# An attention GNN on one core: h joins the ff sum by transposes between the first down products, b2 as a 128-row product, and the mask's diagonal as a column

## The reference, cut to what matters

```python
x0 = relu(layernorm(x))                      # L0's input
mask = adj + eye(n) > 0
for l in range(3):
    scores = leaky(si[:, :, None] + sj[:, None, :] + attn_b[l], 0.2)   # si = x @ w[:d], sj = x @ w[d:]
    attn = softmax(where(mask, scores, -inf))
    h = layernorm(x + attn @ x, g1[l], beta1[l])
    ff = gelu(h @ W1[l] + b1[l]) @ W2[l] + b2[l]                       # hidden width 1024
    x = layernorm(h + ff, g2[l], beta2[l])
x = x_in + x
h = relu(layernorm(x)); Wh = h @ W
e = where(adj > 0, leaky(s_i[:, :, None] + s_j[:, None, :], 0.2), -9e15)   # without the eye
out = x + leaky(softmax(e, axis=1) @ Wh)
```

## Time and profile before

| | |
|---|---|
| median of 3 runs | 2426.69 us |
| span of the profiled execution | 2423.8 us (no time of its own is given for it; the median lies 2.9 us above its span) |
| TensorE busy | 2089.5 us, 86% |
| VectorE busy | 1850.2 us, 76% |
| ACT busy | 1086.6 us, 45% |
| GpSimd busy | 926.1 us, 38% |
| DMA | 52.85 MB, mean 22 GB/s |

### The profile page before, as it was taken

The page is one execution under the profiler, slowest core; times in us unless marked ns, Lnnn a source line. Parts: engine busy times, 40 slices in busy tenths (PEclk is TensorE's granted clock), DMA queues, the critical chain, the costliest instruction groups (busy, mean ns, idle before and its releaser), DMA issues.

```text
span 2423.8 us, 34901 instructions
## 1 busy us (share of the span) xinstructions
PE 2089.5 (86%) x11649; PEld 1778.6 (73%) x11649; DVE 1850.2 (76%) x4984; ACT 1086.6 (45%) x1668; POOL 926.1 (38%) x658
## 2 busy tenths in 40 slices
PE   3898888988899988999889988899888998889894
PEld 2777677877778766877767776778767786778783
DVE  6777887778787787777878778786788768877755
ACT  3444454434454445534444444544445444544341
POOL 2444433443344343343334333343334334333442
PEclk9899999999999999989999899989989999899997
DMA  4001100001000010000100010000100001000000
GB/s 139 18 18 44 43 4 12 14 18 44 11 18 1 18 44 11 18 1 27 36 10 18 1 53 11 10 18 8 46 10 9 18 18 40 5 13 23 1 1 18
DMA packets 40522, 52.85 MB, mean 22 GB/s; under 512 B 2906, under 2 KB 30852, under 8 KB 40324
## 3 DMA queue, kind: packets, MB, share of 16 engines
q1 hardware_dynamic: 40324, 50.37, 6.5%
HBM read 41.97 MB, written 8.39 MB: 21 GB/s over the span
## 4 chain that ended last, share of the span: by engine, by line
issue 34%; PE 27%; DVE 21%; POOL 15%; ACT 2%; DMA 0%; POOLq 0%; SPq 0%; DVEq 0%; ACTq 0%
PE ps_a L400 8%; PE ps_d L469 7%; PE ps_u L439 6%; POOL gelu_lo L1158 5%; DVE h_last L815 4%; DVE h_last L817 4%; POOL rstd L1125 3%; DVE normed L922 3%; PE ps_a L499 2%; POOL probs L1164 2%; PE ps_t L357 2%; DVE probs L966 2%; POOL normed L1141 1%; POOL x_res L1143 1%; POOL x_res L1150 1%
## 5 line engine op out<-in xcount | busy, mean ns | idle before, releaser
L666 ACT ACTIVATE g_full<-ps_u,vec_col 128x512 f32<-128x512 f32 x384 | 259.2, 687 | 782.5 <-PE ps_u L439 349.6
L469 PE MATMUL ps_d<-w_hi,gelu_hi 128*128 128x256 f32 x1536 | 483.4, 315 | 1.2 <-DVE gelu_lo L902 1.1
L469 PE MATMUL ps_d<-w_lo,gelu_hi 128*128 128x256 f32 x1536 | 458.3, 298 | 0.0
L469 PE MATMUL ps_d<-w_hi,gelu_lo 128*128 128x256 f32 x1536 | 457.6, 298 | 0.0
L1125 POOL TENSOR_TENSOR rstd<-var_eps,minus_half 128x4 f32<-128x4 f32 x128 | 136.9, 1069 | 683.4 <-DVE var_eps L787 683.4
L400 PE MATMUL ps_a<-x_nat,probs 128*128 128x257 f32 x1536 | 365.8, 390 | 32.6 <-DVE normed L869 27.7
L1158 POOL TENSOR_TENSOR gelu_lo<-g_full,gelu_hi 128x512 fp32r<-128x512 f32 x240 | 318.7, 1337 | 171.4 <-ACT gelu_hi L674 161.8
L400 PEld LDWEIGHTS ps_a<-x_nat,probs 128*128 128x128 f32 x1536 | 285.0, 191 | 106.8 <-DVE normed L869 34.1
L469 PEld LDWEIGHTS ps_d<-w_hi,gelu_hi 128*128 128x128 f32 x1536 | 320.7, 209 | 19.1 <-DVE gelu_lo L902 3.8
L469 PEld LDWEIGHTS ps_d<-w_lo,gelu_hi 128*128 128x128 f32 x1536 | 322.4, 210 | 7.0
L469 PEld LDWEIGHTS ps_d<-w_hi,gelu_lo 128*128 128x128 f32 x1536 | 321.5, 209 | 0.0
(11 more groups left out here) (133 smaller groups left out, 4223.8 us busy)
## 6 DMA issues: line engine op xcount, KB each, us to landing
adj_in<-adj_dram SPq DMA_DIRECT2D x64, 256.0 KB, 3.1
x_nat<-x_dram SPq DMA_DIRECT2D x16, 512.0 KB, 4.1
x_res<-x_dram SPq DMA_DIRECT2D x16, 512.0 KB, 4.0
out_dram<-x_res SPq DMA_DIRECT2D x64, 128.0 KB, 1.7
x_res<-L_gnn_W_dram SPq DMA_DIRECT2D x5, 1024.0 KB, 5.6
probs<-L_gnn_W_dram SPq DMA_DIRECT2D x1, 1024.0 KB, 8.9
attn_row<-L_gnn_attn_w_dram SPq DMA_DIRECT2D x1, 768.0 KB
g_row<-L_gnn_g_dram SPq DMA_DIRECT2D x1, 384.0 KB
```

The lines of the kernel that those rows point to most:

```text
L469: last = pe.matmul(ps_d[c // 2][:, cols:cols + D], h[:, r, tok], w[:, layer, f, :], start=False, stop=(f == FC - 1 and i == 2), skip_group ...
L666: full = act.activation(g_full[:, f % 2, :], ps_u[f % 2][:, :], ACT.Gelu, bias=b1_col[:, layer, f:f + 1])
```

## The change

`residual` becomes one chunk's work and is called between the chunks of the first down product, behind the wait for gelu_lo. h comes from h_full by two transposes (f32, one pass each). ones_r and b2_parts have 128 rows, of which two are not zero in ones_r. The diagonal's transposes and copies go; VectorE takes the diagonal as a column instead, by a multiply-reduce with the identity, clears it by a multiply, and final_mask adds it back. A column of side 1 is kept by a copy in slots (2,1). `junk` gets memory of its own.

```diff
-        b2_parts = sb("b2_parts", [2, LAYERS, D], F32R)
-        ones_r = sb("ones_r", [2, P], F32R)
+        b2_parts = sb("b2_parts", [P, LAYERS, D], F32R)
+        ones_r = sb("ones_r", [P, P], F32R)
+        off_diag = sb("off_diag", [P, P], BF16)
...
-        junk = h_last[:, :, :].rearrange("p k n -> p (k n)").bitcast(BF16)
+        junk = sb("junk", [P, NC * N], BF16)
...
-                (b2_two, b2.rearrange("(o l) d -> o l d", o=1).broadcast_to([2, LAYERS, D])),
+                (b2_all, b2.rearrange("(o l) d -> o l d", o=1).broadcast_to([P, LAYERS, D])),
...
-                    if begun(self_added.at(g, c - 1)):
-                        sp.wait_ge(self_added.sem, self_added.at(g, c - 1))
+                    if begun(adj_read.at(g, c - 1)):
+                        sp.wait_ge(adj_read.sem, adj_read.at(g, c - 1))
...
+            def residual(n, layer, c):
+
+                if c % 2 == 0 and begun(ln2_apply.at(n - 1)):
+                    pe.wait_ge(ln2_apply.sem, ln2_apply.at(n - 1, c // 2 + 1))
+                cols = (c % 2) * D
+                dst = ps_d[c // 2]
+                for k in range(KC):
+                    pe.matmul(dst[:, cols + k * P:cols + (k + 1) * P], h_full[:, k, c * P:(c + 1) * P], ident[:, :],
+                              start=(c % 2 == 0 and k == 0), stop=False, is_transpose=True, skip_group_check=True)
+                pe.matmul(dst[:, cols:cols + D], ones_r[:, :], b2_parts[:, layer, :], start=False, stop=False,
+                          skip_group_check=True)
 
             def down(n, layer, f):
-                if f == 0:
-                    residual(n, layer)
                 by, turn = lo_turn(f)
                 pe.wait_ge(lo_done[by].sem, lo_done[by].at(n, turn))
                 r = f % RING
                 for c in range(NC):
+                    if f == 0:
+                        residual(n, layer, c)
...
-                    mask_transposes(prepare, 0, (4,), ps_a[0])
-                    pe.wait_ge(mask_ready.sem, mask_ready.at(prepare, NC))
+                    pe.wait_ge(mask_ready.sem, mask_ready.at(prepare))
...
-                    mask_transposes(graph_a, 1, (4,))
...
-                    if masks_x is not None:
-                        mask_copies(masks_x, 0, (4,), ps_a[0])
...
-                    dve.tensor_scalar(diag_nat[:, c, :], adj_in[:, c % 2, blk], 0.0, MASKED, ALU.is_le, ALU.mult)
-                    dve.tensor_tensor(adj_self[:, :], adj_in[:, c % 2, blk], ident[:, :], ALU.add).then_inc(self_added.sem, 1)
-                    dve.wait_ge(self_added.sem, self_added.at(g, c + 1))
-                    dve.tensor_scalar(mask_nat[:, side, c, blk], adj_self[:, :], 0.0, MASKED,
-                                      ALU.is_le, ALU.mult).then_inc(nat_ready.sem, 1)
+                    dve.wait_ge(adj_read.sem, adj_read.at(g, c + 1))
+                    dve.tensor_tensor_reduce(junk[:, c * P:(c + 1) * P], mask_nat[:, side, c, blk], ident_b[:, :], 1.0, 0.0, ALU.mult,
+                                             ALU.add, diag_mask[:, side, c:c + 1])
+                    dve.tensor_tensor(mask_nat[:, side, c, blk], mask_nat[:, side, c, blk], off_diag[:, :],
+                                      ALU.mult).then_inc(nat_ready.sem, 1)
...
-                    last = dve.tensor_copy(mask_g[:, c, c * P:(c + 1) * P], diag_t[:, side, c, :])
+                    last = dve.scalar_tensor_tensor(out=mask_g[:, c, blk], in0=ident_b[:, :], scalar=diag[:, c:c + 1],
+                                                    in1=mask_t[:, side, c, blk], op0=ALU.mult, op1=ALU.add)
...
+            def keep_diagonal(pair):
+                dve.tensor_copy(diag_kept[:, :], diag_mask[:, 1, :]).then_inc(diag_saved.sem, 1)
+                dve.wait_ge(diag_saved.sem, diag_saved.at(pair))
...
-            step(dve.tensor_copy(ident_r[:, :], ident[:, :]))
...
+            pool.memset(all_ones, 1.0)
...
+            pool.affine_select(out=ones_f, in_=ones_f, compare_op=ALU.is_ge, fill=0.0,
+                               base=1, pattern=[[0, P]], channel_multiplier=-1)
...
-            pool.tensor_copy(ident_b[:, :], ident[:, :]).then_inc(consts.sem, 1)
+            pool.tensor_copy(ident_b[:, :], ident[:, :])
+            pool.tensor_tensor(off_diag[:, :], all_ones, ident[:, :], ALU.subtract).then_inc(consts.sem, 1)
```

More of the change, by code:

```diff
@@ L359, in columns_to_rows, with mask_transposes @@
                 return last
-            def mask_transposes(g, side, chunks, bank=None):
+            def mask_transposes(g, side, chunks):
                 for c in chunks:
-                    view = (ps_t[c % 2] if bank is None else bank)[:, :].bitcast(BF16)
+                    view = ps_t[c % 2][:, :].bitcast(BF16)
                     if c >= 2:
                         pe.wait_ge(mask_ready.sem, mask_ready.at(g, c - 1))
-                    if c < NC:
-                        pe.wait_ge(nat_ready.sem, nat_ready.at(g, c + 1))
+                    pe.wait_ge(nat_ready.sem, nat_ready.at(g, c + 1))
                     for j in range(NC):
-                        block = mask_nat[:, side, c, j * P:(j + 1) * P] if c < NC else diag_nat[:, j, :]
-                        last = pe.transpose(view[:, j * P:(j + 1) * P], block, ident_b[:, :])
+                        last = pe.transpose(view[:, j * P:(j + 1) * P], mask_nat[:, side, c, j * P:(j + 1) * P],
+                                            ident_b[:, :])
                     last.then_inc(mask_pe.sem, 1)
@@ L441, in up @@
                 last.then_inc(u_done.sem, 1)
-            def residual(n, layer):
-                for c in range(NC):
-                    if c % 2 == 0 and begun(ln2_apply.at(n - 1)):
-                        pe.wait_ge(ln2_apply.sem, ln2_apply.at(n - 1, c // 2 + 1))
-                    cols = (c % 2) * D
-                    dst = ps_d[c // 2]
-                    for k in range(KC):
-                        for i, h in enumerate((h_hi, h_lo)):
-                            pe.matmul(dst[:, cols + k * P:cols + (k + 1) * P], h[:, k, c * P:(c + 1) * P],
-                                      ident_r[:, :], start=(c % 2 == 0 and k == 0 and i == 0), stop=False,
-                                      skip_group_check=True)
-                    pe.matmul(dst[:, cols:cols + D], ones_r[:, :], b2_parts[:, layer, :], start=False, stop=False,
-                              skip_group_check=True)
+            def residual(n, layer, c):
[8 more added lines that the diff above has]
+                          skip_group_check=True)
             def down(n, layer, f):
-                if f == 0:
-                    residual(n, layer)
                 by, turn = lo_turn(f)
@@ L1066, in pair_body @@
                         prepare_x(graph_a, other, pair + side, n if late is None else None, late)
+                    if layer == LAST and side == 1:
+                        keep_diagonal(pair)
                     if prepare is not None and side == 1:
```

57 lines of the change are left out of this document (28 added, 29 removed).

## The result

The kernel after takes 2446.51 us (median of four runs, 2445.70 to 2448.52) against 2426.41 us of the kernel before: ratio 1.0083, 95% interval 1.0069 to 1.0097, 20 us slower. The forecast was 2450.0 us. The span of its profiled execution is 2444.0 us against 2423.8, so the two traces show the same 20 us.

A forecast was written before the change was run, and what follows sets the result against it. VectorE was taken to set the pace up to s_j, TensorE after it, slowed by half clock after pauses. Terms summed to +26.2 us, cut to +24; 2423.8 + 24 + 2.9 gave about 2450 us, 8-in-10 range 2415 to 2472.

The forecast's parts named there:

- The block: Between the first down products: 0.40 us a chunk, 1.6 us a slot, taking 91 us off TensorE in 48 blocks.
- value at s_j: At TensorE's wait for VectorE's column ahead of L357: the saved time only lengthens the pause, worth zero.
- (a): Slots (0,0): longer pause before L499 lowers the clock; 2.3 us in 5 of 7 slots, +11.5 us.
- (b): Slots (0,1): longer pause makes L499 dearer by 1.4 us (0.9 to 2.9) in seven slots, +10 us.
- (c): The other 33 slots with a pause already pay half clock after L357; +0.1 us each, +3 us.
- The masks: Mask work: chunks -2 us beside GpSimd in (2,0), final_mask +3, keep_diagonal +1.6, input_apply -2; diagonal's transposes zero.
- rival (1): Slots (2,0) and (2,1): mask instructions slip in ahead of GpSimd, -3.2 us in each of 14, about 2406; chance 0.17.
- terms for keep_diagonal and input_apply: keep_diagonal: copy and wait ahead of s_j, 8 times, +1.6 us; input_apply in (0,0) earlier, 7 slots, -2 us.
- The setup: Ahead of the last small load: b2 on 128 rows adds 378 KB at 336 GB/s, +1.1 us.
- The tail: End of the run: no gain forecast; final_mask's +0.4 us counted there once.
- (2): Layer-0 slots: pauses grow but the clock costs no more, about 2428 us; chance 0.15.
- (3): Half clock after L357 lasts 5.6 us everywhere, +0.8 us in 33 slots, about 2476 us; chance 0.08.

The follow-up runs named there:

- experiment 1: The kernel before with the mask part of the change alone, its block staying the old one; 2439.47 us, ratio 1.0067.
- Experiment 6: Three kernels: the kernel after plus 16 zero products a slot, 2436.24 us; that plus the lost transposes, 2438.05; mask part alone plus those transposes, 2437.02 us.
- experiment 5: The kernel after plus 35, 26, 26 and 44 unused transposes of the identity at four places; 2374.21 us, ratio 0.9788.
- e10_b2_two_rows: The kernel after with b2 loaded and multiplied as two rows again, as before the change; 2445.56 us, ratio 1.0088.

## Why the prediction was right, and which steps were not

**The block** was taken at 0.40 us a chunk and measured 0.34 (0.14 for two transposes, 0.20 for the b2 product). The value at s_j was zero, as said; L357 still starts as s_j ends. TensorE's busy time fell by 111 us, where 60 to 80 was said, and the pause before L357 in (1,0) is 5.48 us, just past the 5.4 said.

**The sum.** The forecast was +24 and the traces differ by 20.2 us, but this closeness is in part luck: (a) and (b) together came to 27.8 us where 21.5 was taken, and all else to -7.6 where +2.7 was taken.

**(a) Slots (0,0)**, 2.3 us in 5 of 7: measured +2.4 to +3.1 in these five, 13.5 us, and +0.4 and +0.2 in the two that had the fall already. The step "the fall needn't cover all 16 products" was the wrong caution: it covers them.

**(b) Slots (0,1)**, 1.4 us in 7: measured +2.45 in each of six and -1.0 in the last, 13.7 us against 10. The term was mis-sized by its choice between ends: the row nearest by place (8.67 us for 32 products) is of the last pair, whose fall is a short one in nine of the eleven kernels that fall there (8.2 to 8.7 us for the 32). After the change the same slot has a pause of 4.73 us in place of 2.81, and still 8.64 us for the 32 products. The upper end, 2.9, was nearer.

**(c) The other slots with a pause**, +0.1 each: measured less than zero. Half clock behind L357 went from 5.7 to 3.95 us in (1,0) and from 4.55 to 3.5 in (1,1), as in the longer pause more of it passes while TensorE stands still; (1,0) and (1,1) gained 3.3 us in the loop. The bound of -0.6 held it, the value taken did not. The reading behind it, half clock as the price of the pause of 2.53 us, was wrong for this slot: the clock had fallen before that pause began.

**The masks.** Here a step failed: every term of the mask part was priced by its own time (+0.6 us in all; the diagonal's transposes, inside the pause of (0,0), at zero), and none by what it does to pauses and clock. By experiment 1 the mask part alone brings the fall and 16 us. Experiment 6 shows that these transposes by themselves are not the reason. The forecast held because the fall is paid once, whichever part causes it: luck, as far as this step goes. In (2,0) the chunk beside GpSimd got cheaper by more than the 0.3 us taken: 0.55 us a slot with the mask part alone (285.5 to 282.2 us). The timeline of VectorE and GpSimd beside the earlier trace rows:

```profile
1160.28 2.35 DVE L784 CUSTOM_DVE_ANT_0 junk<-mask_nat,ident_b 128x128 bf16<-128x128 bf16 x1
...
1162.56 0.22 DVE L786 TENSOR_TENSOR mask_nat<-mask_nat,off_diag 128x128 bf16<-128x128 bf16 x1
...
1159.84 2.64 POOL L1146 TENSOR_TENSOR x_res<-x_res,beta_row 128x1024 f32<-128x1024 f32 x1
```

One instruction is held to the end of GpSimd's, where two were, so rival (1) did not come about. The four operations of final_mask take 1.14 us for 0.50: +0.64, where 0.4 was taken (and four at 0.2 each for 0.50 would have been +0.3). The terms for keep_diagonal and input_apply were not separated.

**The setup**, +1.1 (b2 is 3 KB a row, 6 KB in two rows): the first slot begins 2.7 us later and bias_col is waited for to 20.28 us, not 17.26. One profile overstates it. Over the eight kernels with b2 on 128 rows VectorE's first dot starts at 18.90 to 20.28 (mean 19.7), over the six with two rows at 16.64 to 18.73 (mean 17.7): 2.0 us. The division of bytes by 336 GB/s gave half of it; why the load cost more, no run shows.

**The tail** was taken at zero, and the last slot and tail gained 3.4 us. In the last slot there is no s_j to wait for, and VectorE's stretch of four instructions (L945 before, L933 after) began 2.05 us sooner after the slot's start. And beside GpSimd it took 3.33 us and not 5.41:

```profile
2349.05 5.41 DVE L945 TENSOR_SCALAR wh<-x_res,mean,rstd 128x256 f32<-128x256 f32 x4 [1.13 <-POOL rstd L1125]
...
2370.58 3.33 DVE L933 TENSOR_SCALAR wh<-x_res,mean,rstd 128x256 f32<-128x256 f32 x4 [1.13 <-POOL rstd L1121]
```

Which part gave the 3.4 us isn't shown: the mask part alone, with the old block, gained 2.9 there, and over the fourteen kernels last slot and tail take 87.5 to 94.1 us without a clear order.

**Rivals.** (2), that the pauses grow and the clock costs nothing: every pause of 3 us or more in (0,0) was paid for. (3): half clock after L357 got shorter, not longer, and its reason, that transposes don't count, fell with experiment 5. The rule of the Trainium skill, "TensorE: Matmul & The Clock Gate", section "HAM oscillation", was the right one to weigh: by it (a) would have been 2.9 in five slots, and 2.4 to 3.1 was measured. But not every pause was priced alike: the slots (0,0) with 1.1 to 2.75 us before the change paid nothing.

## What to carry to other kernels

Taking work from TensorE ahead of a wait is not free, though the engine only waits longer: look at what it does right behind the wait, and at the granted clock there. In the slots (0,0) the price came as a step and not by the pause's length, so the parts did not add up (16, 20, and 20 us together), and putting one part's transposes back gave back next to nothing (2437 us after 2439). Time each part alone before adding prices, and look for half clock ahead of the wait too, as it sets the pause as much as the work does. Where a wait for another engine can't be shortened, unused work ahead of it (8 to 30 transposes) made the kernel before 1.9% faster; with the change and b2 in two rows (26 to 44 of them, leaving 0 to 2.2 us of pause) it was 2.3%. The real saving of 111 us of TensorE's time, without such fill, made it 0.8% slower.

## What was not expected of the hardware

- A spell of 1.2 GHz ahead of a wait is useful: the kernel before has it in six of seven slots (0,1), and no fall behind the wait there. Sixteen unused products and four transposes a slot don't bring it back (2438 us, not 2424).
- Single-pass transposes of float32 between pauses keep the clock at 1.00 in most slots, as products do (2374 and 2390 us).
- A VectorE instruction on 128 x 4 elements took 4.48 us beside a GpSimd instruction of 4.51 us in the setup; the same one took 0.16 us in the kernel after, where it started 0.04 us ahead of it.
- A two-row product of 256 columns isn't cheaper than one of 128 rows. In the same place, between transposes and products of 128 rows, it took a mean of 394 ns (e10_b2_two_rows) against 366, and a chunk of the block grew by 0.40 us.
